# A mixture-of-experts kernel: the adapter's second product contracts over 128 rows, 96 of them zero, in place of 32

## The reference

```python
for k in range(K):
    ...
    h = gelu(jnp.einsum('ecd,edf->ecf', buf, w1) + b1[:, None, :])
    y = jnp.einsum('ecf,efd->ecd', h, w2) + b2[:, None, :]
    a = jnp.einsum('ecr,erd->ecd', gelu(jnp.einsum('ecd,edr->ecr', buf, wd)), wu)
    y = y + a
    tok = y[e, jnp.minimum(pos_c, cap - 1)]
    out = out + tok * keep[:, None].astype(x.dtype) * w[:, None]
sh = gelu(xt @ sw1 + sb1) @ sw2 + sb2
sh = sh + gelu(xt @ swd) @ swu
out = out + 0.2 * sh
```

## Time and profile before

| | |
|---|---|
| median of 3 runs | 2028.45 us (2028.31 to 2029.46) |
| the profiled execution's own time | 2026.92 us |
| its span, first to last instruction | 2025.2 us |
| mean granted TensorE clock | 0.988 |
| busy: PE, PEld, DVE, ACT, POOL | 96%, 80%, 56%, 49%, 16% |
| busy DMA share and rate from 1724.4 to 1969.5 us (experts 1 to 6) | 0.60 to 0.61, 224 to 226 GB/s |

### The profile page before, as it was taken

The page is one execution under the profiler, slowest core; times in us unless marked ns, Lnnn a source line. Parts: engine busy times, 40 slices in busy tenths (PEclk is TensorE's granted clock), DMA queues, the critical chain, the costliest instruction groups (busy, mean ns, idle before and its releaser), DMA issues. The chain is left out here.

```text
span 2025.2 us, 32167 instructions
## 1 busy us (share of the span) xinstructions
PE 1945.5 (96%) x10292; PEld 1611.8 (80%) x10292; DVE 1131.0 (56%) x2516; ACT 983.2 (49%) x2076; POOL 316.4 (16%) x252
## 2 busy tenths in 40 slices
PE   7899999999999999999999999999788999999998
PEld 5787888888888778878888888887553688999997
DVE  3457677677677665767677677766766530000002
ACT  3303776676577571066677577667254441121111
POOL 0300111211211113011211211122233200000001
PEclk9999999999999999999999999999899899999998
DMA  6652111111111155411111111113100907666442
GB/s 208 205 190 71 37 45 45 48 33 49 44 31 41 40 184 188 135 35 40 50 36 44 44 32 48 36 31 115 32 0 21 341 0 258 223 257 247 181 182 65
DMA packets 122798, 198.08 MB, mean 98 GB/s; under 512 B 12205, under 2 KB 61541, under 8 KB 118624
## 3 DMA queue, kind: packets, MB, share of 16 engines
q1 hardware_dynamic: 118768, 188.59, 28.0%
q10 hardware_dynamic: 2672, 4.55, 0.7%
q0 software_dynamic: 1280, 3.93, 0.6%
HBM read 151.50 MB, written 45.81 MB: 97 GB/s over the span
## 5 line engine op out<-in xcount | busy, mean ns | idle before, releaser
L747 DVE TENSOR_TENSOR crs_ptl<-crs_tp,crs_pth 128x512 fp32r<-128x512 f32 x512 | 352.6, 689 | 178.2 <-ACT crs_pth L587 177.8
L587 ACT ACTIVATE crs_pth<-crs_tp 128x512 fp32r<-128x512 f32 x504 | 301.6, 599 | 244.6 <-PE crs_tp L960 241.4
L511 POOL TENSOR_TENSOR crs_vl<-crs_vraw,crs_vh 128x512 fp32r<-128x512 f32 x128 | 165.1, 1290 | 1081.0 <-ACT crs_vh L594 1081.0
L951 PE MATMUL crs_ring<-crs_kh,crs_ql 128*128 128x512 f32 x512 | 233.9, 457 | 0.0
L970 PE MATMUL crs_ov<-crs_ptl,crs_vh 128*128 128x512 f32 x512 | 209.6, 409 | 9.7 <-DVE crs_ptl L747 8.8
L970 PE MATMUL crs_ov<-crs_pth,crs_vh 128*128 128x512 f32 x512 | 202.2, 395 | 0.0
L951 PE MATMUL crs_ring<-crs_kh,crs_qh 128*128 128x512 f32 x512 | 201.5, 394 | 0.0
L951 PE MATMUL crs_ring<-crs_kl,crs_qh 128*128 128x512 f32 x512 | 200.9, 392 | 0.0
L970 PE MATMUL crs_ov<-crs_pth,crs_vl 128*128 128x512 f32 x512 | 200.1, 391 | 0.0
L576 ACT ACTIVATE crs_prob<-crs_prob,crs_nmax 128x512 f32<-128x512 f32 (+1 forms) x192 | 166.2, 867 | 65.4 <-DVE crs_nmax L762 65.4
L960 PE MATMUL crs_tp<-all_ident,crs_prob 128*128 128x128 f32 x1024 | 195.1, 272 | 3.0 <-ACT crs_more L576 3.0
(11 more groups left out here) (268 smaller groups left out, 3407.9 us busy)
## 6 DMA issues: line engine op xcount, KB each, us to landing
moe_w<-in_L_ffn_w SPq DMA_DIRECT2D x48, 1024.0 KB, 13.0
v_scratch<-crs_more SPq DMA_DIRECT2D x64, 512.0 KB, 2.9
crs_vraw<-v_scratch SPq DMA_DIRECT2D x128, 256.0 KB, 2.7
ex_w<-in_L_ffn_w SPq DMA_DIRECT2D x16, 1024.0 KB, 13.7
crs_prob<-in_ctx SPq DMA_DIRECT2D x16, 512.0 KB, 4.7
crs_wo<-in_L_xattn_Wo SPq DMA_DIRECT2D x16, 512.0 KB, 4.2
moe_w<-in_L_ffn_sw SPq DMA_DIRECT2D x8, 1024.0 KB, 13.6
qry_wq<-in_L_xattn_Wq SPq DMA_DIRECT2D x16, 256.0 KB, 3.8
```

Of the source, the lines that this page charges most:

```text
L511: nc.gpsimd.tensor_tensor(vl[:, n % VR, :, :], vraw[:, :, :], vh[:, n % VR, :, :].bitcast(F32), ALU.subtract).then_inc(s["v_lo"], 1)
L587: act.activation(pth[:, k % PT, :], tp[k % PT][:, :], ACT.Copy).then_inc(s["pt_hi"], 1)
L747: v.tensor_tensor(ptl[:, k % PT, :], tp[k % PT][:, :], pth[:, k % PT, :].bitcast(F32), ALU.subtract).then_inc(s["pt_lo"], 1)
L951: m = pe.matmul(ring[at % RING][:, :], a[:, t // RT, rows], w[:, n % KR, :], start=i == 0, stop=i == 2)
```

## The change

`wu` and `rT` have 128 partitions in place of 32. Their loads, ScalarE's GELU into `rT`, and the shared adapter's matmul (L1924) name the first 32 partitions and are as before. The 17th matmul of each output chunk (L1990 before, L1994 after) reads as it did, `wu[i][:, ...]` and `rT[:, :]`, so it now contracts over all 128 partitions. Partitions 32 to 127 of both buffers of `wu` and of `rT` are zeroed once, by six memsets on VectorE.

```diff
@@ -1434,7 +1434,8 @@
         wd = [t.sb(f"wd_{i}", [P, KC, R]) for i in range(2)]
-        wu = [t.sb(f"wu_{i}", [R, D]) for i in range(2)]
+
+        wu = [t.sb(f"wu_{i}", [P, D]) for i in range(2)]
         gate = t.sb("gate", [P, KC, E])
@@ -1454,7 +1455,7 @@
         bufT = t.sb("bufT", [P, 2, KC, SL])
-        rT = t.sb("rT", [R, SL])
+        rT = t.sb("rT", [P, SL])
 
@@ -1505,13 +1506,13 @@
-                    sp.dma_start(wu[1][:, :], a["L0_ffn_swu"]).then_inc(s["sad_ld"], 16)
+                    sp.dma_start(wu[1][0:R, :], a["L0_ffn_swu"]).then_inc(s["sad_ld"], 16)
...
-                sp.dma_start(wu[i][:, :], a["L0_ffn_wu"][bass.ds(e, 1), :, :].rearrange("o r n -> (o r) n")).then_inc(ad_ld[i], 16)
+                sp.dma_start(wu[i][0:R, :], a["L0_ffn_wu"][bass.ds(e, 1), :, :].rearrange("o r n -> (o r) n")).then_inc(ad_ld[i], 16)
@@ -1652,6 +1653,9 @@
             shared(0, 0, FC)
             shared(1, 1, FC - 1)
 
+            for z in (*wu, rT):
+                for part in (slice(R, 2 * R), slice(2 * R, P)):
+                    v.memset(z[part, :], 0.0)
             v.wait_ge(s["exp_ok"], 2)
@@ -1820,7 +1824,7 @@
                 act.wait_ge(s["r_ps"], e + 1)
-                act.activation(rT[:, :], bank[6][0:R, 0:SL], ACT.Gelu)
+                act.activation(rT[0:R, :], bank[6][0:R, 0:SL], ACT.Gelu)
@@ -1921,7 +1925,7 @@
             for i in OUT_ORDER:
-                pe.matmul(bank[2 + i][:, :], rS[:, i * P:(i + 1) * P], wu[1][:, :], start=False, stop=True).then_inc(s["so_ps"], 1)
+                pe.matmul(bank[2 + i][:, :], rS[:, i * P:(i + 1) * P], wu[1][0:R, :], start=False, stop=True).then_inc(s["so_ps"], 1)
```

## The result

The changed kernel takes 2014.54 us in the median of four runs (2013.35 to 2018.14), the kernel before beside it 2028.95 us (2028.31 to 2029.57). The ratio is 0.9932, 95% interval [0.9915, 0.9949]: 14.4 us less. The profiled execution takes 2013.35 us, its span is 2011.6 us. Ratios in this document are taken over fast runs alone: one slow execution, of 3982.76 us, fell to the variant with wd on the full tile, where it is in the median (2014.61 us without it), and nothing on record shows its cause.

The account below looks back on a forecast made before the run. TensorE, busy 96% of the span, was taken to set the pace. Tile changes gone save 12.7 us, memsets and the rest cost 0: 2028.45 - 12.7 = 2015.8 us, range 2013.6 to 2019.5.

Parts of the forecast that it names:

- the sum: Whole kernel: 31 chunks at 0.404 us give 12.5 us, the last chunk 0.2 us, together 12.7 us off.
- The chunk: Layer 2 of each expert: an output chunk's 34 instructions take 4.60 us in place of 5.01, 0.404 us less.
- the gapless run's pace: Layer 1 of expert 1: 64 full-array weight loads without a gap, 0.1354 us from start to start.
- the lower end: Layer 2 chunks counted by the chain at 0.139 us an instruction: 4.72 us a chunk, gain 9.1 us.
- a part only: Rival A, 5%: gaps go, but the padded pair or what follows keeps some delay; gain 9.1 us, 2019.3 us.
- The tile as cause: Around L1990 and L1976: idle gaps stand where the tile changes; three steps about L1990 cost 0.81 us, should cost 0.41.
- eight accumulations without a gap: Layer 1 of expert 1: gapless loads pass eight accumulations' ends and change PSUM bank, so neither makes the gap.
- The memsets: Six on VectorE before the gate weights: 2.5 us, bounds 1.1 and 3.4, hidden by its 5.76 us wait; cost 0.
- The threshold of 6.3 us: Memsets ahead of the routing: TensorE would lose what goes beyond 5.76 + 0.56 = 6.3 us.
- What is late next: Experts shorten to 39.2 us without new weight waits; VectorE's final wait for TensorE falls from 7.03 to 5.4 us.
- Slower: Rival C, 2%: a 128-row load at L1990 can't overlap the preceding stream; 5.3 us more, 2033.7 us.
- No change: Rival B, 3%: the gap belongs to L1990's 17th place, not its tile; within 0.2%, 2028.4 us.

Follow-up runs that it names:

- the second comparison: The unchanged changed kernel measured once more, beside the variant with the full-tile wd: 2017.60 us, ratio to the kernel before 0.9950 [0.9933, 0.9966].

## Why the prediction was right

The forecast was 2015.8 us, the measured median 2014.54, inside the range. That the time is so close is in part luck: the medians of one and the same change lay 14.4 and 11.3 us below the kernel before in two comparisons, on either side of the 12.7 of the sum. What carries the forecast is its mechanism, read in the stretch that was changed.

- *The chunk.* 34 steps of the gapless run's pace gave 4.60 us; it is 4.61, and the experts' stretch lost 12.43 us against 12.7 of the sum. Reading the pace from load starts was the choice that mattered: the chain's 0.139 us a step, the lower end, would have given 9.1. That rival, a part only, is gone with it.
- *The tile as cause.* The argument from eight accumulations without a gap held. The wide buffers and the zeros, unused, give nothing; 64 rows give nothing, 96 all, at the same place in the accumulation. The prediction's wording, that the gap stands where the tile changes, was too wide: a row that prints 96\*128, 80\*128 or 128\*80 behind full ones has no gap.
- *The memsets.* 2.9 us, between the 2.5 taken and the bound of 3.4, under a wait that became 2.60 us. The kernel with unused zeros prices them at nothing that can be measured. The threshold of 6.3 us was about right as well (9.2 us of them gave a stall of 3.1), but the price beyond it was too low: the prediction charged TensorE what goes beyond, and it paid 1.6 us for the clock too.
- *What is late next.* An expert took 39.3 us (1761.57 to 1800.91), no wait for a DMA came up at its head, and VectorE waited 5.63 us at the last expert's end, against 5.4 worked out.
- *The rest.* 1.2 us of the 13.6 between the spans are outside the experts' stretch. With the same program run again these parts came out otherwise (layer norm at 1567.29, the last stretch 14.94 us): they are no part of the change, and the second comparison's 11.3 us lies 1.4 us below the sum, the first's 14.4 lies 1.7 above it.
- *Slower*, since a 128-row load could not be overlapped: in the changed trace loads of 0.190 us on one and the same tile start every 0.136 us. For loads that follow one another on the full tile the measurement decides against the rule quoted from the Trainium skill; the same section also lets a load run ahead into a background weight buffer, and with that the rows agree.
- *No change*, since 32 rows take the time of 128: the single instructions agree with that rule (loads of 182, 184, 191 and 190 ns at 32, 64, 96 and 128 rows, and an ordinary step inside the excursion). What it leaves out is the way there and back. That is told by another page of the Trainium skill, "TensorEngine Tiling (Array Packing)", section "Tiling Modes": changing the mode, not just the tile, drains TensorE; and it lists modes of 32 and 64 rows and of 32 and 64 columns. The runs agree in every point tried: 32 and 64 rows and 32 columns pay, 96 and 128 do not. That a drain is what fills the 0.40 us is the page's word; the runs show only the price.

## What to carry to other kernels

Look for weight loads of a smaller tile between full ones, and read the distance of starts about them, since busy time hides the gap. Here each excursion to a smaller tile cost 0.3 to 0.4 us beyond its instructions. Operands padded with zeros to 96 or 128 rows, or to 128 columns, removed it where TensorE sets the pace (64 columns were not tried), and putting two small matmuls behind one another halved it. All of this was measured with float32 operands and 160 columns moving. Put the memsets under a wait that exists, and know how long it is: here a stall of TensorE of 3.1 us cost 4.7 in that place.

## What the runs showed of the hardware

- The price of an excursion is the same for 32 and for 64 rows, and for two instructions in it as for four: 0.46 us from load to load for two, 0.73 for four, which is two ordinary steps more.
- A matmul over 96 rows and transposes with 80 columns stand among full ones without a gap, and transposes over 80 rows follow full loads without one.
- A stall of 3.1 us in the middle of dense matmuls was followed by steps at a mean granted clock of 0.54; with the 1.6 us that these lost it cost 4.7 us.
- The layer norm of `experts` began, in the same program, at 1563.89 us in one profile and at 1567.29 in another. A difference of a few us between two kernels has to be read in the stretch that was changed, where the two profiles of the change agree to 0.01 us.
